# Routed FFN: fixed blocks for each expert's first 128 rows, the last two loads of w2 behind the last transpose

## The chip, the cores and the metric

One core of a Trainium2 chip. The metric is the device time of one execution in microseconds (us). The engines: PE (TensorE), DVE (VectorE), ACT (ScalarE), POOL (GpSimd) and SP (SyncE), which here only issues DMAs and waits.

## What is computed

The reference is a layer with a cross attention and a routed feed-forward part, for 1024 rows x of 128 values and 6404 rows of context. Cut to what matters:

```python
cq = jnp.einsum('bcd,bqd,d->bcq', c, q, w_cq) + b_cq          # c = layernorm(x), q = context
s = (c @ w_c + b_c)[:, :, None] + (q @ w_q + b_q)[:, None, :] + cq
a = jax.nn.softmax(s, axis=2)
c2q = jnp.einsum('bcq,bqd->bcd', a, q)
b_att = jax.nn.softmax(jnp.max(s, axis=2), axis=1)
q2c = jnp.einsum('bc,bcd->bd', b_att, c)[:, None, :]
x = x + jnp.concatenate([c, c2q, c * c2q, c * q2c], axis=-1) @ W_l.T + b_l
y = layernorm(x)
expert_id = argmax(y @ wr + br)                                # 8 experts, one for each row
out = x + (gelu(y @ w1[expert] + b1[expert]) @ w2[expert] + b2[expert])   # 128 -> 512 -> 128
```

## The kernel before, in words

**Attention.** The 1024 rows are 8 tiles of 128 (T = 8). Of each tile the 6404 scores are worked off in 7 pieces of 1024 columns (the last of 260). All products run in fp16 with a high and a low part, so that each operand is split in two. For a piece PE makes the scores (`scores`, L1059 to L1061), DVE takes them out of PSUM with their maximum (L800), ACT makes the exponential (L651) and its fp16 high part (`high`, L666), DVE or, for piece 3 of a tile, POOL makes the low part (`low`, L817; `low_piece`, L533), SP issues a DMA transpose of both parts (`transpose`, L393), and PE multiplies the transposed piece with the context (`weighted`, L1079 and L1081). Four buffers hold pieces under way; ACT's high part waits until the transpose of the piece four before it has landed.

**Weights.** w1 and w2 are loaded in 4 DMAs each of 512 KB (`load_w1`, `load_w2`). SP issues them between transposes: `W1_BEHIND` and `W2_BEHIND` name the tile and piece behind which. The loads of w2 stand behind pieces (2,5), (3,3), (4,1) and (4,5). POOL makes the high and low part of each of the 8 loads: `split(n)` has 4 casts (L570) and 4 subtractions (L574) of 128x256, placed behind its low piece of a tile by `splits`; the semaphore `w_low` counts the splits that are done.

**Behind the last transpose** SP writes an empty slot into every row of a DRAM buffer `xs` (14 blocks of 128 rows x 257 words, 5 DMAs, L431: "fills"); `slots_emptied` counts them.

**Routing** of the first 7 tiles (TA = 7). PE makes the router's scores, DVE the best expert of each row (`best`, L930 to L941), PE the rank of a row within its expert and the count of each expert, and DVE from them, in a chain in which every instruction waits for the one before (`link`), the slot of each row: L947 to L957, which ends with `pos_ready`. Each expert's rows fill whole blocks of 128, one expert behind the other, so 14 blocks (NB = 14) suffice whatever the counts, and which expert a block has is known only at run time. Then DVE normalises the last tile (`normalise`, L743 to L762). POOL waits for the fills and for `pos_ready` (L599, L600) and sends the 7 tiles' rows to their slots with 7 indirect DMAs (L602), counted by `rows_sent`. SP waits for that (L456) and reads the blocks back in 4 batches (`block_rows`, L449: the normalised halves first, the rest separately).

**The feed-forward part** has 22 blocks of 128 rows, in a fixed order. 8 of them are "dense": the last tile's 128 rows go through all 8 experts, with a mask, because they need no routing. They stand at places 0 to 4, 10, 16 and 21 (`DENSE_AT`); the 14 routed ("sent") blocks fill the other places (`SENT_AT`), the first of them at place 5. A dense block k takes its weights from the array `wp`. For a sent block SP reads the block's expert into a register and copies that expert's 512 KB from `wp` to a buffer (`fetch`, L444, SBUF to SBUF), the first two before the rows are read and the others among the reads. PE goes through the blocks: `up` (16 matmuls, L1276 to L1279), ACT's two Gelus (L710, L711), DVE's low part (L985), `down` (L1290 to L1296), DVE's sum (`finish_half` and `finish`). `up` is issued two blocks ahead. Before the first sent block's `up`, PE transposes the first batch of rows (`turn(0)`, L1245), ACT and DVE split it (L700, L977). PE waits for all splits (L1303) before the first dense block. POOL sends each sent block's result to `out` with an indirect DMA (L608) and at the end waits for all (L612); SP writes the last tile (L476) and waits for that (L477).

Of the kernel before, what the change touches and what calls it, by code (L numbers as in the profile page):

```python
# [24 lines left out]
F16 = mybir.dt.float16  # L25
I32 = mybir.dt.int32
# [7 lines left out]
def build(nc, x, ctxT, w3, b3, wlT, b_l, wr, br, w1, b1, w2, b2, out):  # L34
# [47 lines left out]
    with es:  # L82
# [6 lines left out]
        tri = sb("tri", [P, E, E])  # L89
# [52 lines left out]
        kedge = sb("kedge", [P, E, TA])  # L142
        slot_no = sb("slot_no", [P, NB, E])
        row_no = sb("row_no", [P, 1])
        token = sb("token", [P, T], I32)
        wc2 = gh[:, 0:2 * D].bitcast(F32)
        x_re = stageT[:, XRE:XRE + N].rearrange("p (t d) -> p t d", d=D)
# [3 lines left out]
        ints = stageT[:, XRE - NB * E:XRE].bitcast(I32)  # L151
# [17 lines left out]
        more = carve(E * TA).rearrange("p (a b) -> p a b", b=TA)  # L169
        below = carve(E * E).rearrange("p (a b) -> p a b", b=E)  # L170
        rank = carve(TA * E).rearrange("p (a b) -> p a b", b=E)
        cand = carve(T * E).rearrange("p (a b) -> p a b", b=E)
        mask = carve(E)
        chosen = carve(NB // 2, F16)
        past = carve(NB * E).rearrange("p (a b) -> p a b", b=E)
        oneh = carve(TA * E // 2, F16).rearrange("p (a b) -> p a b", b=E)
        nblk, sblk, eblk = carve(E), carve(E), carve(E)
        posf, rmx, bexpf = carve(TA), carve(T), carve(NB)
        pos, bexp = carve(TA, I32), carve(NB, I32)
# [11 lines left out]
        y7 = stageT[:, (NB + RING) * D:(NB + RING + E) * D].rearrange("p (e d) -> p e d", d=D)  # L191
# [70 lines left out]
        w_low = sem("w_low")  # L262
        b12_landed = sem("b12_landed")
# [9 lines left out]
        block_w_landed = [sem(f"block_w_landed{k}") for k in range(WSLOTS)]  # L273
# [87 lines left out]
        def block_w(b):  # L361

            k = b % WSLOTS
            return spare[k // (WSLOTS // 2)][:, k % (WSLOTS // 2) * 4 * F:(k % (WSLOTS // 2) + 1) * 4 * F]\
                .rearrange("p (a f) -> p a f", f=F)

        @block.sync
        def _(sp):
# [50 lines left out]
            W2_BEHIND = {(2, 5): 0, (3, 3): 1, (4, 1): 2, (4, 5): 3}  # L419
# [7 lines left out]

            sp.wait_ge(empty_ready, 2)
# [34 lines left out]
            fetch(4)  # L463
# [9 lines left out]
            for b in range(10, NB):  # L473
                fetch(b)
# [874 lines left out]
```

## Time and profile before

| | us |
|---|---|
| median of 3 runs | 234.27 |
| lowest and highest | 232.66 and 235.13 |
| the profiled execution's own time | 234.39 |
| its span, first to last instruction | 232.7 |
| busy in it: PE, DVE, ACT, POOL | 201.1, 180.6, 157.9, 128.6 |

The profile is of one execution. Times in its rows are us from the start of the span; an instruction's line is that of kernel.py. The span is shorter than the execution by what lies around it, 1.7 us. "Granted clock" is TensorE's: 1.00 stands for 2.4 GHz, 0.50 for 1.2 GHz. PE's busy time is of pipelined matmuls and says little by itself: what counts in each stretch is which wait ends last.

### The profile page before, as it was taken

Reading aid. Unit: us, or ns where it says so; the run is one execution under the profiler, and the core shown is the slowest. Engines: PE = TensorE matmul, PEld = TensorE weight load, DVE = VectorE, ACT = ScalarE, POOL = GpSimd, SP = SyncE. Lnnn points to the kernel's source line nnn. Section 1 sums busy time; section 2 is a strip of 40 time slices with the busy share of each in tenths; the row PEclk is TensorE's granted clock in tenths of the full one; section 3 lists DMA queues with packets and bytes.
Section 4 is the critical chain, followed back from the end, with each engine's and each line's share of the span. In section 5 each row is a group of like instructions: output and inputs, shape, how many; then the busy total and the mean of one; then the engine's idle time right before and its main releaser. Section 6 shows DMA issues by size and latency. Waiting matters only on the chain.

```text
span 232.7 us, 5011 instructions
## 1 busy us (share of the span) xinstructions
PE 201.1 (86%) x1837; PEld 150.3 (65%) x1837; DVE 180.6 (78%) x395; ACT 157.9 (68%) x249; POOL 128.6 (55%) x177
## 2 busy tenths in 40 slices
PE   0379969999999999989989899899993797999980
PEld 0133417776766767757666566789973686899970
DVE  2899797697998998998995997958756435776872
ACT  2752899399399699699595799689531445667650
POOL 3695718807915807978508947744400740066763
PEclk9999985899999999999999999999996569999998
DMA  6999979899999999999999999988994369999200
GB/s 215 389 251 263 226 223 237 192 234 174 220 215 216 278 230 269 241 198 233 216 213 256 184 220 258 201 196 185 239 263 121 120 219 290 346 370 378 98 11 12
DMA packets 142958, 51.78 MB, mean 223 GB/s; under 512 B 121172, under 2 KB 140773, under 8 KB 142934
## 3 DMA queue, kind: packets, MB, share of 16 engines
q1 hardware_dynamic: 142000, 50.08, 93.2%
q0 software_dynamic: 784, 1.38, 1.7%
q8 instruction: 14, 0.23, 0.4%
q14 instruction: 10, 0.08, 0.1%
q10 hardware_dynamic: 150, 0.00, 0.0%
HBM read 10.74 MB, written 3.75 MB: 62 GB/s over the span
## 4 chain that ended last, share of the span: by engine, by line
PE 49%; DVE 21%; DMA 11%; issue 8%; ACT 4%; POOL 3%; SPq 2%; DVEq 0%; POOLq 0%
DMA PT<-Phl 10%; PE psX L1079 5%; PE psS L1061 5%; PE psO L1079 5%; PE psS L1060 5%; PE psS L1059 5%; DVE S L800 5%; DVE Phl L817 3%; PE psS L1290 3%; PE psX L1081 3%; PE psO L1081 3%; ACT S L651 3%; SPq L393 2%; PE psS L1276 2%; PE psS L1296 2%
## 5 line engine op out<-in xcount | busy, mean ns | idle before, releaser
L651 ACT ACTIVATE S<-S,negb 128x1024 f32<-128x1024 f32 x48 | 55.1, 1147 | 18.4 <-DVE negb L808 18.4
L800 DVE TENSOR_SCALAR_CACHE_REDUCE S<-psS 128x1024 f32<-128x1024 f32 x48 | 58.2, 1217 | 11.4 <-PE psS L1061 11.2
L817 DVE TENSOR_TENSOR Phl<-S,Phl 128x1024 f16<-128x1024 f32 x38 | 51.5, 1355 | 5.0 <-ACT Phl L666 4.8
L533 POOL TENSOR_TENSOR Phl<-S,Phl 128x256 f16<-128x256 f32 x40 | 26.3, 689 | 51.7 <-ACT Phl L666 51.7
L666 ACT CAST Phl<-S 128x1024 f16<-128x1024 f32 x48 | 50.3, 1047 | 5.2 <-DMA PT<-Phl 3.7
L1059 PE MATMUL psS<-qT,gh 128*128 128x512 f16 x96 | 37.7, 393 | 5.4 <-DVE S L800 2.6
L1079 PE MATMUL psX<-qn,PT 128*128 128x256 f16 x204 | 36.4, 273 | 2.1 <-DMA PT<-Phl 2.1
L1079 PE MATMUL psO<-qn,PT 128*128 128x256 f16 x204 | 37.3, 276 | 0.9 <-DMA PT<-Phl 0.8
L1061 PE MATMUL psS<-qT,gl 128*128 128x512 f16 x96 | 37.9, 395 | 0.0
L1060 PE MATMUL psS<-qT,gh 128*128 128x512 f16 x96 | 37.9, 394 | 0.0
L1081 PE MATMUL psO<-qn,PT 128*128 128x128 f16 x204 | 35.7, 221 | 0.0
L1081 PE MATMUL psX<-qn,PT 128*128 128x128 f16 x204 | 35.0, 219 | 0.0
L608 POOL DMA_INDIRECT out_x<-stageT,S x14 | 17.7, 1265 | 22.1 <-DVE stageT L1011 17.1
L1079 PEld LDWEIGHTS psX<-qn,PT 128*128 128x128 f16 x204 | 20.0, 98 | 7.5 <-DMA PT<-Phl 3.5
L1079 PEld LDWEIGHTS psO<-qn,PT 128*128 128x128 f16 x204 | 20.3, 99 | 6.3 <-DMA PT<-Phl 1.9
L710 ACT ACTIVATE Phl<-psS 128x512 f16<-128x512 f32 x22 | 13.2, 598 | 15.4 <-PE psS L1279 9.0
L1081 PEld LDWEIGHTS psO<-qn,PT 128*128 128x128 f16 x204 | 20.2, 99 | 2.2 <-issue 0.3
L1081 PEld LDWEIGHTS psX<-qn,PT 128*128 128x128 f16 x204 | 20.0, 98 | 1.9
L1059 PEld LDWEIGHTS psS<-qT,gh 128*128 128x128 f16 x96 | 9.8, 102 | 14.6 <-DVE S L800 3.5
L1061 PEld LDWEIGHTS psS<-qT,gl 128*128 128x128 f16 x96 | 9.7, 101 | 12.1 <-issue 1.4
L985 DVE TENSOR_TENSOR Phl<-Phl 128x512 f16<-128x512 f32 x22 | 15.0, 682 | 2.4 <-issue 2.4
L574 POOL TENSOR_TENSOR wp<-wp 128x256 f16<-128x256 f32 x16 | 15.6, 1005 | 0.3
(239 smaller groups left out, 425.3 us busy)
## 6 DMA issues: line engine op xcount, KB each, us to landing
PT<-wp SPq DMA_DIRECT2D x8, 512.0 KB, 6.0
stageT<-in_ctxT SPq DMA_DIRECT2D x6, 512.0 KB, 7.0
qn<-wp SPq DMA_DIRECT2D x6, 512.0 KB, 7.3
wp<-in_w SPq DMA_DIRECT2D x4, 512.0 KB, 4.9
stageT<-in_w SPq DMA_DIRECT2D x4, 512.0 KB, 4.9
rows_by_expert<-stageT SPq DMA_DIRECT2D x4, 385.5 KB, 5.6
PT<-Phl SPq DMA_TRANSPOSE x48, 4.2
S<-rows_by_expert SPq DMA_DIRECT2D x2, 258.0 KB, 5.4
```

What stands on the lines that cost most here:

```text
L533: last = nc.gpsimd.tensor_tensor(lo[:, r], slot(t, e)[:, r], hi[:, r], ALU.subtract)
L574: last = nc.gpsimd.tensor_tensor(parts[:, 1, at + a:at + a + CHUNK], src[:, a:a + CHUNK], parts[:, 0, at + a:at + a + CHUNK], ALU.subtract)
L608: pool.indirect_dma_start(out=out, out_offset=bass.IndirectOffsetOnAxis(ap=rows[:, b, 2 * D:ROW].bitcast(I32), axis=0), in_=yf[:, b, :], i ...
L651: nc.scalar.activation(slot(t, e), slot(t, e), ACT.Exp, bias=negb[:, t:t + 1], accum_out=Lp[:, t * NG + e:t * NG + e + 1]).then_inc(exp_do ...
L666: nc.scalar.copy(hi, slot(t, e)).then_inc(high_done, 1)
L800: nc.vector.tensor_scalar(out=into, in0=bank(u, n)[:, 0:into.shape[1]], scalar1=1.0 / GS, scalar2=None, op0=ALU.mult, op1=ALU.max, accum_o ...
L817: nc.vector.tensor_tensor(lo, slot(t, e), hi, ALU.subtract).then_inc(low_done, 1)
L1059: nc.tensor.matmul(dst, g_h, hi, start=True, stop=False)
L1060: nc.tensor.matmul(dst, g_h, lo, start=False, stop=False)
L1061: last = nc.tensor.matmul(dst, g_l, hi, start=False, stop=True)
L1079: nc.tensor.matmul(acc[:, 0:2 * D].rearrange("p (a d) -> p a d", a=2), PT[:, 2 * e * TW + i, :], both[:, :, i, :], start=(j == 0), stop=Fa ...
L1081: last = nc.tensor.matmul(acc[:, 0:D], PT[:, 2 * e * TW + n + i, :], both[:, 0, i, :], start=False, stop=(j == QT - 1), skip_group_check=True)
```

## The change

Each expert's first 128 rows get a block of their own, at a fixed place: the first 8 sent blocks are those of experts 0 to 7, and take their weights and biases from where the dense blocks take them. The rows of an expert beyond 128 go to 6 further blocks (NX = 6), for which the expert is found and its weights are fetched as before; 14 sent blocks and 22 blocks remain. So 6 fetches are left of 14, each with a buffer of its own, and they come behind the first batches of rows. A row's slot is now its rank plus 128 times its expert, or, from rank 128 on, plus the expert's shift: the DVE chain from the counts to `pos_ready` is longer for this.

The loads 2 and 3 of w2 leave tile 4 and are issued behind the last transpose, ahead of the fills; load 2 goes to the place of `c_sb`, hence SP's wait for `q2c_in_psum`. Their high parts are made by ACT, in two casts of 128x1024 behind the transposed rows' copies (L687); their low parts by POOL, 4 subtractions each, the one ahead of the scatters of rows (and of the waits in front of them), the other behind them. POOL's other splits move: one in each of the tiles 1 to 6. PE waits for the four loads of w1 before the first dense block, and in `down` for the load of w2 that it uses. Of the dense blocks the one at place 16 moves to place 20, so that the last two blocks are dense and the sent ones end with place 19.

The core of the diff (renamed buffers, constants' patterns and the reuse of `y7` left out):

```diff
@@ -51,13 +51,12 @@
-    NB = TA + E - 1
+    NX = TA - 1
+    NB = E + NX
...
-    DENSE_AT = (0, 1, 2, 3, 4, 10, 16, 21)
+    DENSE_AT = (0, 1, 2, 3, 4, 10, 20, 21)
...
-    ROUTE_CONSTS = 19
-    WSLOTS = 12
-    FIRST = 2
+    ROUTE_CONSTS = 21
@@ -358,11 +360,14 @@
-def block_w(b):
-    k = b % WSLOTS
-    return spare[k // (WSLOTS // 2)][:, k % (WSLOTS // 2) * 4 * F:(k % (WSLOTS // 2) + 1) * 4 * F]\
-        .rearrange("p (a f) -> p a f", f=F)
+def w2_stage(k):
+    return c_flat if k == H - 2 else stageT[:, k * WC:(k + 1) * WC]
+def block_w(k):
+    half = (NX + 1) // 2
+    return spare[k // half][:, k % half * 4 * F:(k % half + 1) * 4 * F].rearrange("p (a f) -> p a f", f=F)
...
 def _(sp):
@@ -401,7 +406,7 @@
     def load_w2(k):
...
-        sp.dma_start(stageT[:, k * WC:(k + 1) * WC].rearrange("p (e k d) -> p e k d", k=FC, d=D),
+        sp.dma_start(w2_stage(k).rearrange("p (e k d) -> p e k d", k=FC, d=D),
@@ -416,7 +421,7 @@
-    W2_BEHIND = {(2, 5): 0, (3, 3): 1, (4, 1): 2, (4, 5): 3}
+    W2_BEHIND = {(2, 5): 0, (3, 3): 1}
@@ -425,23 +430,23 @@
+    sp.wait_ge(q2c_in_psum, 1)
+    load_w2(H - 2)
+    load_w2(H - 1)
...
-    expert_reg = [sp.alloc_register(f"expert{j}") for j in range(NB)]
-    sp.wait_ge(w_low, T)
+    expert_reg = [sp.alloc_register(f"expert{j}") for j in range(NX)]
...
-    sp.reg_load(expert_reg[0:FIRST], bexp[0:1, 0:FIRST])
-    ex = [sp.snap(r, min_val=0, max_val=E - 1) for r in expert_reg[0:FIRST]]
-    def fetch(b):
-        if b >= WSLOTS:
-            sp.wait_ge(y_in_psum, SENT_AT[b - WSLOTS] + 1)
-        sp.dma_start(block_w(b), wp[:, :, bass.ds(ex[b] * F, F)]).then_inc(block_w_landed[b % WSLOTS], 16)
+    sp.reg_load(expert_reg[0:NX], bexp[0:1, 0:NX])
+    ex = [sp.snap(r, min_val=0, max_val=E - 1) for r in expert_reg]
+    def fetch(k):
+        sp.dma_start(block_w(k), wp[:, :, bass.ds(ex[k] * F, F)]).then_inc(block_w_landed[k], 16)
     def block_rows(g, a, b, done):
@@ -449,31 +454,23 @@
-    for b in range(FIRST):
-        fetch(b)
-    sp.reg_load(expert_reg[FIRST:NB], bexp[0:1, FIRST:NB])
-    ex += [sp.snap(r, min_val=0, max_val=E - 1) for r in expert_reg[FIRST:NB]]
...
     block_rows(0, 0, D, rows_landed)
     block_rows(1, 0, D, rows_landed)
+    block_rows(0, D, ROW, rest_landed)
+    block_rows(1, D, ROW, rest_landed)
+    block_rows(2, 0, D, rows_landed)
+    sp.wait_ge(w_low, T)
+    fetch(0)
+    block_rows(2, D, ROW, rest_landed)
+    fetch(1)
+    block_rows(3, 0, D, rows_landed)
...
-    block_rows(0, D, ROW, rest_landed)
-    fetch(3)
-    block_rows(1, D, ROW, rest_landed)
-    fetch(4)
-    fetch(5)
-    block_rows(2, 0, D, rows_landed)
-    fetch(6)
-    block_rows(2, D, ROW, rest_landed)
-    fetch(7)
-    fetch(8)
-    block_rows(3, 0, D, rows_landed)
-    fetch(9)
     block_rows(3, D, ROW, rest_landed)
-    for b in range(10, NB):
-        fetch(b)
+    for k in range(3, NX):
+        fetch(k)
...
-    sp.dma_start(out[TA * P:N, :], y7[:, E - 1, :]).then_inc(out7_landed, 16)
+    sp.dma_start(out[TA * P:N, :], y7[:, (E - 1) % 2, :]).then_inc(out7_landed, 16)
@@ -559,6 +557,19 @@
+    def low_half(n, parts, src, at):
+        for a in range(0, WC, CHUNK):
+            last = nc.gpsimd.tensor_tensor(parts[:, 1, at + a:at + a + CHUNK], src[:, a:a + CHUNK],
+                                           parts[:, 0, at + a:at + a + CHUNK], ALU.subtract)
+        last.then_inc(w_low, 1)
+    def split_late(n):
+        at = (n - H) * WC
+        pool.wait_ge(w_high_late, n - T + 3)
+        low_half(n, w2p, w2_stage(n - H), at)
     def split(n):
@@ -582,7 +590,7 @@
     split(0)
-    splits = {2: (1,), 3: (2, 3), 4: (4,), 5: (5, 6), 6: (7,)}
+    splits = {2: (1,), 3: (2,), 4: (3,), 5: (4,), 6: (5,)}
@@ -595,12 +603,14 @@
+    split_late(T - 2)
     pool.wait_ge(tokens_ready, 1)
...
     for t in range(TA):
         pool.indirect_dma_start(out=xs, out_offset=bass.IndirectOffsetOnAxis(ap=pos[:, t:t + 1], axis=0),
...
+    split_late(T - 1)
@@ -685,6 +695,11 @@
+    for n in (T - 2, T - 1):
+        at = (n - H) * WC
+        act.wait_ge(w_landed[n], 16)
+        act.wait_ge(w_low, H)
+        nc.scalar.copy(w2p[:, 0, at:at + WC], w2_stage(n - H)).then_inc(w_high_late, 1)
     deviation(4, TA, T)
@@ -943,24 +958,30 @@
+    link(nc.vector.tensor_copy(extra[:, E:E + 1], ones[:, 0:1]))
...
-    link(nc.vector.tensor_tensor(more[:, :, :], count_psum.unsqueeze(2).broadcast_to([P, E, TA]),
+    link(nc.vector.tensor_tensor(more[:, :, :], count_psum.unsqueeze(2).broadcast_to([P, E, NX]),
...
-    link(nc.vector.tensor_reduce(out=nblk[:, :], in_=more[:, :, :], axis=AX.X, op=ALU.add))
+    link(nc.vector.tensor_reduce(out=extra[:, 0:E], in_=more[:, :, :], axis=AX.X, op=ALU.add))
...
-                                 nblk[:, :].unsqueeze(1).broadcast_to([P, E, E]), ALU.mult))
-    link(nc.vector.tensor_reduce(out=sblk[:, :], in_=below[:, :, :], axis=AX.X, op=ALU.add))
-    link(nc.vector.tensor_tensor(rank[:, :, :], rank_psum.rearrange("p (t e) -> p t e", e=E),
-                                 sblk[:, :].unsqueeze(1).broadcast_to([P, TA, E]), ALU.add))
+                                 extra[:, :].unsqueeze(1).broadcast_to([P, E, E + 1]), ALU.mult))
+    link(nc.vector.tensor_reduce(out=shift[:, :], in_=below[:, :, :], axis=AX.X, op=ALU.add))
+    ranks = rank_psum.rearrange("p (t e) -> p t e", e=E)
+    link(nc.vector.scalar_tensor_tensor(out=over[:, :, :], in0=ranks, scalar=float(P),
+                                        in1=shift[:, :].unsqueeze(1).broadcast_to([P, TA, E]),
+                                        op0=ALU.is_ge, op1=ALU.mult))
+    link(nc.vector.scalar_tensor_tensor(out=rank[:, :, :], in0=iob.broadcast_to([P, TA, E]), scalar=float(P),
+                                        in1=ranks, op0=ALU.mult, op1=ALU.add))
+    link(nc.vector.tensor_tensor(rank[:, :, :], rank[:, :, :], over[:, :, :], ALU.add))
...
     normalise(x1, x2n, TA, T, x2n_ready)
-    link(nc.vector.scalar_tensor_tensor(out=eblk[:, :], in0=nblk[:, :], scalar=float(P), in1=sblk[:, :],
+    link(nc.vector.scalar_tensor_tensor(out=eblk[:, :], in0=extra[:, 0:E], scalar=float(P), in1=shift[:, :],
...
-    link(nc.vector.tensor_tensor(past[:, :, :], eblk[:, :].unsqueeze(1).broadcast_to([P, NB, E]),
+    link(nc.vector.tensor_tensor(past[:, :, :], eblk[:, :].unsqueeze(1).broadcast_to([P, NX, E]),
@@ -1247,16 +1268,13 @@
     def weights(b):
-        if b in SENT_AT:
-            return block_w(SENT_AT.index(b))
-        k = DENSE_AT.index(b)
-        return wp[:, :, k * F:(k + 1) * F]
+        j = SENT_AT.index(b) if b in SENT_AT else DENSE_AT.index(b)
+        return wp[:, :, j * F:(j + 1) * F] if j < E else block_w(j - E)
     def bias_rows(b):
-        if b in SENT_AT:
-            return chosen[:, SENT_AT.index(b):SENT_AT.index(b) + 1].broadcast_to([P, P])
-        return pick[:, DENSE_AT.index(b), :]
+        j = SENT_AT.index(b) if b in SENT_AT else DENSE_AT.index(b)
+        return pick[:, j, :] if j < E else chosen[:, j - E:j - E + 1].broadcast_to([P, P])
     def up(b):
@@ -1264,8 +1282,9 @@
-            pe.wait_ge(block_w_landed[j % WSLOTS], 16 * (j // WSLOTS + 1))
-            pe.wait_ge(chosen_rows, 1)
+            if j >= E:
+                pe.wait_ge(block_w_landed[j - E], 16)
+                pe.wait_ge(chosen_rows, 1)
@@ -1286,6 +1305,8 @@
         pe.wait_ge(h_high, b + 1)
+        j = SENT_AT.index(b) if b in SENT_AT else DENSE_AT.index(b)
+        pe.wait_ge(w_low, H + j // 2 + 1 if j < E else T)
@@ -1300,7 +1321,7 @@
-    pe.wait_ge(w_low, T)
+    pe.wait_ge(w_low, H)
```

## Rows read from the trace of the kernel before

**Rows 1.** The page's first line.
```profile
span 232.7 us, 5011 instructions
```

**Rows 2.** PE's waits from 193 to 229 us, first row (in total, times, longest).
```profile
PE psS L1276 <- DVE S L977: 1.5, 2, 1.2
```

**Rows 3.** Four stretches, each from one tile's maximum to the next tile's.
```profile
core 0: us, PE busy (x) PEld busy (x) DVE busy (x) ACT busy (x) POOL busy (x), PEclk, DMA share, GB/s
79.50:96.11 16.61, 16.61 (x145) 11.76 (x143) 15.80 (x27) 14.17 (x21) 8.68 (x13) 1.00 1.14 244
96.11:113.38 17.27, 16.51 (x141) 11.27 (x138) 15.80 (x27) 14.17 (x21) 15.23 (x22) 1.00 1.11 231
113.38:132.03 18.65, 17.08 (x142) 11.42 (x141) 15.55 (x27) 14.17 (x21) 9.76 (x16) 1.00 1.23 209
132.03:148.63 16.60, 16.18 (x147) 11.97 (x148) 15.04 (x27) 14.17 (x21) 11.71 (x18) 1.00 1.19 234
```

**Rows 4.** The chain that ended last, inside tile 5 (start, us, what).
```profile
126.35 6.06 DMA PT<-Phl
```

**Rows 5.** ACT in order of time, the same place.
```profile
126.52 1.05 ACT L666 CAST Phl<-S 128x1024 f16<-128x1024 f32 x1 [2.68 <-DMA PT<-Phl]
```

**Rows 6.** SP in order of time: last load of w2, last tile's result.
```profile
118.84 0.57 SPq L404 DMA_DIRECT2D stageT<-in_w  x1
...
228.49 0.36 SPq L476 DMA_DIRECT2D out_x<-stageT  x1
```

**Rows 7.** Two stretches (columns as in rows 3): the load of x, the fills.
```profile
2.50:4.10 1.60, 0.00 (x0) 0.00 (x0) 0.00 (x0) 0.83 (x2) 0.54 (x1) 1.00 1.14 350
170.50:176.50 6.00, 5.47 (x50) 4.75 (x47) 2.50 (x12) 1.30 (x3) 0.20 (x1) 0.96 1.06 282
```

**Rows 8.** The fills' issues; us to landing of the last fill and last result.
```profile
L431 SPq DMA_DIRECT2D rows_by_expert<-stageT x5: 481/757/1392, 169.2 to 172.4; - x5
...
rows_by_expert<-stageT SPq DMA_DIRECT2D x1, 257.0 KB, 6.6
...
out_x<-stageT SPq DMA_DIRECT2D x1, 64.0 KB, 1.6
```

**Rows 9.** POOL in order of time: a split's subtractions, first scatter, last result.
```profile
146.30 3.72 POOL L574 TENSOR_TENSOR wp<-stageT,wp 128x256 f16<-128x256 f32 x4
...
180.29 1.21 POOL L602 DMA_INDIRECT rows_by_expert<-qT,S  x1 [9.11 <-DVE S L957]
...
228.33 0.98 POOL L608 DMA_INDIRECT out_x<-stageT,S  x1 [0.31 <-issue]
```

**Rows 10.** DVE in order of time: a small sum, and the chain's slots.
```profile
149.42 0.63 DVE L887 TENSOR_TENSOR Mrow<-mx,row_term 128x8 f32<-128x8 f32 x1
...
177.94 0.23 DVE L950 TENSOR_TENSOR S<-tri,S 128x64 f32<-128x64 f32 x1
...
179.20 0.17 DVE L957 CAST S<-S 128x7 int32<-128x7 f32 x1
```

**Rows 11.** PE in order of time: first dense block, first batch of rows, first sent block.
```profile
182.39 0.27 PE L1276 MATMUL psS<-S,wp 128*128 128x128 f16 x1 [0.84 <-DVE S L966]
...
193.72 0.55 PE L1245 MATMUL psX<-idf,S 128*128 128x128 f32 x3
195.43 0.23 PE L1276 MATMUL psS<-S,PT 128*128 128x128 f16 x1 [1.16 <-DVE S L977]
```

**Rows 12.** Stretches (columns as in rows 3): idle, what followed, dense blocks, idle.
```profile
30.20:32.30 2.10, 0.00 (x0) 0.00 (x0) 2.10 (x4) 2.08 (x3) 0.00 (x0) 1.00 0.35 130
33.00:42.50 9.50, 9.50 (x37) 6.19 (x36) 7.27 (x10) 7.85 (x13) 6.56 (x9) 0.50 1.07 234
...
176.00:189.50 13.50, 8.26 (x74) 7.34 (x74) 6.95 (x34) 4.39 (x9) 7.36 (x7) 0.50 0.47 157
...
193.80:195.40 1.60, 0.47 (x3) 0.23 (x3) 1.57 (x4) 1.10 (x3) 0.00 (x0) 1.00 1.04 346
```

More of the change, by code:

```diff
@@ L141, in build @@
         iota_e = sb("iota_e", [P, E])
-        kedge = sb("kedge", [P, E, TA])
-        slot_no = sb("slot_no", [P, NB, E])
+        kedge = sb("kedge", [P, E, NX])
+        slot_no = sb("slot_no", [P, NX, E])
         row_no = sb("row_no", [P, 1])
@@ L166, in build @@
         rows = carve(NB * ROW).rearrange("p (b w) -> p b w", w=ROW)
-        more = carve(E * TA).rearrange("p (a b) -> p a b", b=TA)
-        below = carve(E * E).rearrange("p (a b) -> p a b", b=E)
+        more = carve(E * NX).rearrange("p (a b) -> p a b", b=NX)
+        below = carve(E * (E + 1)).rearrange("p (a b) -> p a b", b=E + 1)
         rank = carve(TA * E).rearrange("p (a b) -> p a b", b=E)
+        over = carve(TA * E).rearrange("p (a b) -> p a b", b=E)
         cand = carve(T * E).rearrange("p (a b) -> p a b", b=E)
         mask = carve(E)
-        chosen = carve(NB // 2, F16)
-        past = carve(NB * E).rearrange("p (a b) -> p a b", b=E)
+        chosen = carve(NX // 2, F16)
+        past = carve(NX * E).rearrange("p (a b) -> p a b", b=E)
         oneh = carve(TA * E // 2, F16).rearrange("p (a b) -> p a b", b=E)
-        nblk, sblk, eblk = carve(E), carve(E), carve(E)
-        posf, rmx, bexpf = carve(TA), carve(T), carve(NB)
-        pos, bexp = carve(TA, I32), carve(NB, I32)
+        extra, shift, eblk = carve(E + 1), carve(E), carve(E)
+        posf, rmx, bexpf = carve(TA), carve(T), carve(NX)
+        pos, bexp = carve(TA, I32), carve(NX, I32)
         parts_ring = Phl[:, :, :, :].rearrange("p r a w -> p (r a w)")
@@ L272, in build @@
         rest_landed = [sem(f"rest_landed{g}") for g in range(len(BATCHES))]
-        block_w_landed = [sem(f"block_w_landed{k}") for k in range(WSLOTS)]
+        block_w_landed = [sem(f"block_w_landed{k}") for k in range(NX)]
         chosen_rows = sem("chosen_rows")
@@ L514, in _ @@
             numbers(iota_e[:, :], E, [[1, E]])
-            numbers(kedge[:, :, :].rearrange("p e k -> p (e k)"), E * TA, [[0, E], [P, TA]])
-            numbers(slot_no[:, :, :].rearrange("p b e -> p (b e)"), NB * E, [[P, NB], [0, E]])
-            then(nc.gpsimd.memset(tri[:, :, :], float(P)))
-            then(nc.gpsimd.affine_select(out=tri[:, :, :], in_=tri[:, :, :], compare_op=ALU.is_gt, fill=0.0, base=0,
+            numbers(kedge[:, :, :].rearrange("p e k -> p (e k)"), E * NX, [[0, E], [P, NX]], base=P)
+            numbers(slot_no[:, :, :].rearrange("p b e -> p (b e)"), NX * E, [[P, NX], [-P, E]], base=(E - 1) * P)
+            then(nc.gpsimd.memset(tri[:, :, 0:E], float(P)))
+            then(nc.gpsimd.affine_select(out=tri[:, :, 0:E], in_=tri[:, :, 0:E], compare_op=ALU.is_gt, fill=0.0, base=0,
                                          pattern=[[1, E], [-1, E]], channel_multiplier=0))
+            numbers(tri[:, :, E], E, [[-P, E]], base=(E - 1) * P)
             then(nc.gpsimd.memset(ones16[:, :], 1.0))
@@ L572, in split @@
                 pool.wait_ge(w_high, n + 1)
-                for a in range(0, WC, CHUNK):
-                    last = nc.gpsimd.tensor_tensor(parts[:, 1, at + a:at + a + CHUNK], src[:, a:a + CHUNK],
-                                                   parts[:, 0, at + a:at + a + CHUNK], ALU.subtract)
-                last.then_inc(w_low, 1)
+                low_half(n, parts, src, at)
             low_piece(1, 3)
@@ L1013, in finish @@
                 k = DENSE_AT.index(b)
-                nc.vector.scalar_tensor_tensor(out=y7[:, k, :], in0=half, scalar=mask[:, k:k + 1], in1=t,
+                nc.vector.scalar_tensor_tensor(out=y7[:, k % 2, :], in0=half, scalar=mask[:, k:k + 1], in1=t,
                                                op0=ALU.mult, op1=ALU.add).then_inc(y_ready, 1)
```

10 lines of the change are left out of this document (6 added, 4 removed).

## The prediction

> **What bounds the kernel now.** I read the end first. From the first sent block at 195.43 [rows 11] PE goes from block to block until it drains; its waits there [rows 2] are 1.5 us for DVE's split of the row batches, and the view's one other row is 1.0 us for DVE's low part. No row names a transfer: PE never waited for a fetch. So the 8 fetches that fall away give nothing by themselves on PE, and what counts is when that first sent block starts.
>
> It starts when the rows have come. With the last dense block done PE transposes the first batch at 193.72 and then idles 1.16 us for ACT and DVE [rows 11]. The batch is read when the 7 scatters have landed, and these begin at 180.29, 0.9 us after the slots are ready at 179.37 [rows 9, 10]. The fills are close by: the last, issued at 172.4, lands 6.6 us later, at 179.0 [rows 8]. So before the change DVE's chain sets the scatters, by 0.4 us.
>
> Then the loop: from one tile's maximum to the next takes 16.61 and 16.60 us in two stretches and 18.65 in the one that holds the last load of w2 [rows 3, 6]. The chain of waits lies there in a transpose's landing of 6.06 us [rows 4], for which ACT waited 2.68 us [rows 5]: the load stands in the transposes' queue.
>
> **The change part by part.** The sum is made against the profiled execution, 234.39 us (span 232.7 [rows 1] and 1.7 around it); the median is 234.27.
>
> *Loads out of the loop.* Loads 2 and 3 of w2 leave tile 4. The slow stretch should fall to the others' time: 18.65 - 16.60 = 2.05 us. From below: nothing, if the lateness has another cause. From above: 2.7, if the 17.27 of the stretch ahead, which holds load 2, also falls to 16.60 (0.67 more) [rows 3]. I take 2.05, since ACT's 2.68 us wait is a direct witness for the one stretch and I have none for the other. POOL loses one split in the loop, some 6 us, and was not waited for.
>
> *The loads in their new place.* Each of the two issues costs SP 0.57 us [rows 6], which is not the point: the queue is. They stand ahead of the five fills, and the engines are full while the fills run (share 1.06, 282 GB/s [rows 7]). The loads are 1.05 MB. At the rate of the load of x, which also has rows of 512 bytes, 350 GB/s [rows 7], they take 3.0 us; at the fills' own 282, 3.7 us. I take 3.2, near the like transfer. The last fill then lands at 182.2 (182.0 to 182.7) instead of 179.0. From below: nothing, if reads of DRAM and the writes of fills run beside each other.
>
> *The slot chain.* One copy and two operations of 56 elements are added, each as long as its like, some 0.25 us from start to start [rows 10]: 0.75 us. Slots are ready at 180.1. This also delays the last tile's normalisation and so the dense blocks (from 182.39 [rows 11] to 183.1). Both are hidden if the fills come last: POOL waits for both, and the later decides.
>
> *Scatters.* The first begins 0.9 us after the last of its waits, so at 182.2 + 0.9 = 183.1, against 180.29: 2.8 us late. The 7 scatters, the read, the transpose and the split follow at their old pace, so the first sent block is at 198.2. If only the chain counted, it would be 0.75 us.
>
> *ACT's casts.* Two of 1.05 us [rows 5], behind the copies of the transposed rows. The engines are free for the loads from some 170.5 on [rows 7], and at 1.5 to 1.9 us each, with a margin of two for the landing, they are there at 174 and 176; ACT is free again at 177, and its next work, the root for the last tile, comes after the slots at 179.37 [rows 10]. Hidden; were they later, each us past 179.4 would move the dense blocks, which the wait for the rows covers.
>
> *POOL's subtractions.* 3.7 us for four [rows 9]. The first set runs from some 175 to 178.7 and is done before the slots; behind it wait the scatters, not before 182.2. Hidden by the fills; without the fills' delay it would be hidden by 1.4 us. The second set runs behind the scatters, some 192.5 to 196.2. The weights of experts 0 to 5 are complete by then, and PE needs no others up to place 11; place 12, seven blocks behind the first sent one, comes well after 205. SP's fetches wait for it, behind five reads; the first is needed at place 14. Hidden.
>
> A rule bears on the first set. DVE's sum over 8 columns took 0.63 us at 149.42 while POOL's subtractions ran to 150.0, against 0.23 us for 64 columns with POOL idle [rows 9, 10]. The Trainium skill says why (SBUF — State Buffer, section "Who interferes with whom"): a DVE instruction with two inputs in SBUF contends with a GpSimd instruction that reads SBUF, and the second to issue waits for the first. The trace agrees. By it the three or four such operations of DVE's chain before 178.7 would each lose some 0.4 us, an estimate from these rows, and the slots would come at about 181.4; the first scatter would follow at 182.3, still ahead of the fills' 183.1. It makes nothing worse in my sum, and takes most of the gain from the rival in which the fills are not late.
>
> *The end.* Before, the last result of a sent block is issued by POOL at 228.33, for 0.98 us [rows 9]; at the landing time of the last tile's result, 1.6 us [rows 8], it is there at 230.9. The last tile's own, issued at 228.49 [rows 6], is there at 230.1. With both last blocks dense the sent results end a block, some 1.4 us, earlier, and the last tile's is the last: 0.8 us gained at most, nothing if the rest of the end is fixed. I take 0.7.
>
> Sum: 234.39 - 2.05 + 2.8 - 0.7 = 234.44. With the median 0.12 below the profiled execution, about 234.4 us: three terms that nearly cancel. By their ends the forecast's own range is 232.9 (loop 2.7, scatters 2.6, end 0.8 and a little) to 236.9 (loop nothing, late 3.2, end 0.7).
>
> **The rivals.**
>
> *The clock falls in the wait for the rows: slower.* The dense blocks end at 194 to 195, the first batch is transposed at some 196.5, the first sent block starts at 198.2. So PE has about 3 to 4 us with 0.5 us of work in them; before, it had 1.6 us with 0.47 us of work and stayed at 2.4 GHz [rows 12]. After 2.1 us without any work (30.2 to 32.3) it was at 1.2 GHz from 33 to 42.5, and it was low again from 176 to 189.5, with the dense blocks running on it [rows 12]. Against it: the case before stayed high, and the late dense blocks shorten the idle time. Price: at half the clock a block takes twice its time, so half of the time spent low is lost. In the rows the low level lasted for 7 to 10 us of work; 3.4 to 7.2 us low cost 1.7 to 3.6. The time is 236.1 to 238.0; I name 237.2. It decides from some 4.4 us at the low level on: half of that, 2.2 us, lifts the sum over 236.6.
>
> *The fills are not late.* Reads and writes run beside each other, or the loads are through before the fills fill the engines. Then DVE's chain sets the scatters, 0.75 us late: 234.39 - 2.05 + 0.75 - 0.7 = 232.4, and 231.7 with the whole 2.7 us of the loop. For it: the chain is the later one before. Against: the engines are full from 170.5 to 176.5 with fills alone [rows 7], and the margin is 0.4 us.
>
> *The loop gives nothing.* The stretch of 18.65 us comes from the two earlier loads of w2, which stay, and the loads' going only moves the lateness. Then 234.4 + 2.05 = 236.5. Against it: the stretch after it, without loads, takes 16.60 at once.
>
> *The change doesn't do what it says*: if a fixed block's weights came late, PE would wait in a product for the second set of subtractions. By the times above it is 9 us early; I give this no share.
>
> **How the numbers follow.** Forecast 0.40; clock 0.27; fills not late 0.20; loop gives nothing 0.13. A measurement of this kernel tells about 1%, 2.3 us, from no change, so faster is below 231.9 and slower above 236.6. Forecast: 0.05 faster, 0.31 same, 0.04 slower. Clock: 0.01, 0.03, 0.23. Fills: 0.10, 0.10, 0. Loop: 0.01, 0.03, 0.09. Sums: 0.17 faster, 0.47 same, 0.36 slower. The range leaves out less than a tenth at each end: the fills' rival down to 231.6, the clock's up to 238.3.
>
> **What would show it.** Right: the stretch that was 18.65 us is about 16.6; the last fill lands some 3 us later against the slots; POOL's first scatter begins behind the fills' landing and not behind L957's successor; PE's gap in front of the first sent block is longer by 1.5 us or more. The clock's rival: a granted clock of 0.50 after that gap. Wrong: the first scatter 0.9 us after the slots, or the stretch still over 18 us.

## The result, and the profile after

The change takes 249.38 us (median of 4 runs) against 234.63 us beside it: ratio 1.064 (1.056 to 1.072), 14.8 us slower. The forecast of 234.4 us, its range and every rival missed it. (Here and below the ratios leave disturbed runs out, so that one can differ from that of the medians.) The profiled execution took 248.52 us, its span is 246.8.

Page of the kernel after: the granted clock in 40 slices; the chain's shares by engine; two of the costliest groups; the loop's transposes (how many, median us from issue to landing).

```profile
PEclk9999999998999999997999999999998559999997
...
PE 40%; DMA 25%; DVE 17%; SPq 8%; issue 5%; POOL 2%; ACT 2%; DVEq 0%; ACTq 0%; POOLq 0%
...
L676 ACT CAST Phl<-S 128x1024 f16<-128x1024 f32 x48 | 50.2, 1045 | 18.3 <-DMA PT<-Phl 17.1
...
L1100 PE MATMUL psX<-qn,PT 128*128 128x256 f16 x204 | 39.0, 285 | 10.1 <-DMA PT<-Phl 10.1
...
PT<-Phl SPq DMA_TRANSPOSE x48, 4.9
```

The same line of the page before:

```profile
PT<-Phl SPq DMA_TRANSPOSE x48, 4.2
```

The loss is a wait for transposes. ACT's high parts waited 17.1 us for their landing and PE's products in the row shown 10.1 us; before, 3.7 and 2.1. DMA has 25% of the chain (11% before), SP's queue 8% (2%). The clock is not the cause: its mean is 0.952, against 0.944 before.

Timeline of the kernel after, rows of SP, POOL, DVE and PE from the last tile on (start, duration, engine, line, operation; in brackets the idle time ahead and what ended it):

```profile
179.27 1.77 SPq L398 DMA_TRANSPOSE PT<-Ptail  x1
181.09 0.57 SPq L409 DMA_DIRECT2D c_sb<-in_w  x1
181.72 0.57 SPq L409 DMA_DIRECT2D stageT<-in_w  x1
...
191.92 0.17 DVE L978 CAST S<-S 128x7 int32<-128x7 f32 x1
...
196.20 1.21 POOL L611 DMA_INDIRECT rows_by_expert<-qT,S  x1 [6.96 <-DMA rows_by_expert<-stageT]
...
209.24 0.55 PE L1266 MATMUL psX<-idf,S 128*128 128x128 f32 x3 [0.79 <-DMA S<-rows_by_expert]
210.95 0.23 PE L1295 MATMUL psS<-S,wp 128*128 128x128 f16 x1 [1.17 <-DVE S L998]
```

SP is through with the transposes at 181.04 us, before the change at 169.17: 11.9 us, all lost by the end of the loop. Behind it things go in the order that the forecast had. The scatters begin 4.1 us behind the slots, released by the fills ([rows 9, 10]: 0.9 behind, released by DVE); from the slots, 192.09, to the first sent block it is 18.86 us against 16.06, so 2.8 us more. From the first sent block to the end it is 35.85 us against 37.27.

What is odd stands at the start. Windows of both kernels over 16 to 20 us, where SP issues nothing but the transposes of the context and nothing has been changed, then two of the loop's tiles and the first sent blocks after (us; busy time and count for each engine; granted clock, DMA share, GB/s):

```profile
16.00:20.00 4.00, 3.66 (x18) 1.50 (x17) 4.00 (x7) 0.21 (x1) 4.00 (x6) 1.00 1.22 272
```

```profile
16.00:20.00 4.00, 4.00 (x15) 1.57 (x14) 3.22 (x8) 0.20 (x1) 3.86 (x7) 1.00 1.13 219
81.73:101.95 20.22, 17.33 (x143) 11.40 (x141) 15.37 (x27) 14.15 (x21) 8.88 (x14) 1.00 1.10 202
101.95:123.35 21.40, 18.04 (x141) 12.41 (x142) 15.16 (x27) 14.14 (x21) 7.48 (x12) 0.92 1.13 204
...
209.00:213.00 4.00, 2.60 (x32) 2.31 (x33) 1.25 (x3) 2.42 (x5) 0.00 (x0) 1.00 1.13 318
```

The transfer engines are busy throughout in both (share 1.22 and 1.13) and move 219 GB/s instead of 272. A queue order cannot do that ahead of the loop, so I looked for what the diff changes there. It is one number in the kernel's first allocation, `tri = sb("tri", [P, E, E])`, now `[P, E, E + 1]`: 288 bytes per partition instead of 256. (The cut of the diff ahead of the prediction does not show this line.) Allocations follow each other, so wp, qT, qn, S, Phl, PT and stageT, which all began at multiples of 256 bytes, now begin 32 bytes behind one. Theory A: that alone slows the transposes. Theory B: the moved loads, casts and splits upset the loop. Theory C: some of both.

### The profile page after: what moved, and what is told of

Same layout as the page of the kernel before. It is cut to its first block, busy times and chain, and to the rows that moved or that the text cites. A ratio compares the mean times of both kernels' runs of the same rounds, so it can differ in the third digit from the quotient of the medians.

```text
span 246.8 us, 4988 instructions
## 1 busy us (share of the span) xinstructions
PE 201.7 (82%) x1837; PEld 149.2 (60%) x1837; DVE 179.9 (73%) x398; ACT 159.7 (65%) x251; POOL 122.1 (49%) x171
## 2 busy tenths in 40 slices
DMA packets 138734, 47.58 MB, mean 193 GB/s; under 512 B 121044, under 2 KB 136549, under 8 KB 138710
## 4 chain that ended last, share of the span: by engine, by line
PE 40%; DMA 25%; DVE 17%; SPq 8%; issue 5%; POOL 2%; ACT 2%; DVEq 0%; ACTq 0%; POOLq 0%
DMA PT<-Phl 18%; SPq L398 5%; PE psX L1100 5%; DVE S L815 5%; PE psS L1080 5%; PE psS L1081 4%; PE psS L1082 4%; DMA rows_by_expert<-stageT 4%; DVE Phl L832 3%; PE psS L1311 3%; PE psO L1100 3%; PE psX L1102 3%; POOL rows_by_expert L611 2%; ACT Phl L676 2%; PE psS L1317 2%
## 5 line engine op out<-in xcount | busy, mean ns | idle before, releaser
L676 ACT CAST Phl<-S 128x1024 f16<-128x1024 f32 x48 | 50.2, 1045 | 18.3 <-DMA PT<-Phl 17.1
L832 DVE TENSOR_TENSOR Phl<-S,Phl 128x1024 f16<-128x1024 f32 x38 | 49.2, 1295 | 14.4 <-ACT Phl L676 14.4
L1100 PE MATMUL psX<-qn,PT 128*128 128x256 f16 x204 | 39.0, 285 | 10.1 <-DMA PT<-Phl 10.1
L1100 PE MATMUL psO<-qn,PT 128*128 128x256 f16 x204 | 36.8, 273 | 6.0 <-DMA PT<-Phl 6.0
L1102 PE MATMUL psX<-qn,PT 128*128 128x128 f16 x204 | 37.4, 227 | 0.0
L1082 PE MATMUL psS<-qT,gl 128*128 128x512 f16 x96 | 37.3, 389 | 0.0
L1100 PEld LDWEIGHTS psX<-qn,PT 128*128 128x128 f16 x204 | 20.8, 102 | 17.3 <-DMA PT<-Phl 13.0
L1100 PEld LDWEIGHTS psO<-qn,PT 128*128 128x128 f16 x204 | 19.9, 98 | 12.7 <-DMA PT<-Phl 9.1
L618 POOL DMA_INDIRECT out_x<-stageT,S x14 | 16.8, 1200 | 18.1 <-DVE stageT L1032 14.3
L1102 PEld LDWEIGHTS psX<-qn,PT 128*128 128x128 f16 x204 | 20.8, 102 | 1.7
L1102 PEld LDWEIGHTS psO<-qn,PT 128*128 128x128 f16 x204 | 20.0, 98 | 1.6
L1006 DVE TENSOR_TENSOR Phl<-Phl 128x512 f16<-128x512 f32 x22 | 15.9, 722 | 2.5 <-ACT Phl L726 2.5
L1295 PE MATMUL psS<-S,wp 128*128 128x128 f16 x64 | 15.1, 236 | 2.3 <-DVE S L998 1.5
```

The source lines that it names most:

```text
L618: pool.indirect_dma_start(out=out, out_offset=bass.IndirectOffsetOnAxis(ap=rows[:, b, 2 * D:ROW].bitcast(I32), axis=0), in_=yf[:, b, :], i ...
L676: nc.scalar.copy(hi, slot(t, e)).then_inc(high_done, 1)
L832: nc.vector.tensor_tensor(lo, slot(t, e), hi, ALU.subtract).then_inc(low_done, 1)
L1006: nc.vector.tensor_tensor(hp[:, i, 1, :], hf[:, i, :], hp[:, i, 0, :], ALU.subtract).then_inc(h_low, 1)
L1082: last = nc.tensor.matmul(dst, g_l, hi, start=False, stop=True)
L1100: nc.tensor.matmul(acc[:, 0:2 * D].rearrange("p (a d) -> p a d", a=2), PT[:, 2 * e * TW + i, :], both[:, :, i, :], start=(j == 0), stop=Fa ...
```

## The experiments

**Addresses, nothing else.** The pads are unused tensors of 4-byte numbers; the order of work stays. The kernel before, shifted as the change shifts it:

```diff
 tri = sb("tri", [P, E, E])
+sb("pad", [P, 8])
```

> Theory A (addresses): the change made the first tensor of the on-chip memory 32 bytes per partition longer, so every large tensor behind it starts 32 bytes off a multiple of 64, and the DMA transposes that read Phl and qT and write PT and qn are slower for that alone. Then the kernel before, with nothing changed but 32 bytes put behind tri, loses what the change lost up to the last transpose: its last transposes issue near 181 us instead of 169.2, and the time is 234.6 + 11.9 = 246.5 us (243 to 249), ratio 1.05. Theory B (order of work: the moved loads, casts and splits upset the loop): nothing of the order changes here, so 234.6 us, ratio 1.00. Theory C (the loop got slower from both): about half, 240 us.

Measured: 251.07 us, ratio 1.069 (1.061 to 1.077). The whole loss, in a kernel with none of the change. It is 2 us above the range expected, which was made from the loss up to the change's last transpose; here SP is through with the transposes at 184.1 us, not at 181.0.

The changed kernel with everything put back:

```diff
 tri = sb("tri", [P, E, E + 1])
+sb("pad", [P, 56])
```

> The changed kernel with 224 bytes put behind tri, so that every large tensor starts a multiple of 256 bytes from where it started before, as in the kernel before. Theory A: the transposes are at their old pace, the last ones issue at 169.2 - 2 = 167 us, and what is left is the working of the prediction: 234.4 us, ratio 1.00 (0.99 to 1.015). Theory B: the order of work is what slowed the transposes, so 248.5 us and ratio 1.06 stay. Theory C: 241 to 243 us.

Measured: 235.17 us, ratio 1.003 (0.999 to 1.006). With the addresses put back the change is no longer slower. Theories B and C fall.

As in the first, with 16 numbers for 8:

> The kernel before with 64 bytes put behind tri: the large tensors start at an odd multiple of 64. If theory A holds and a multiple of 64 is enough, 234.6 us, ratio 1.00; if it takes a multiple of 256, as all of them have in the kernel before, about as slow as with 32 bytes, 240 to 247 us. Theory B: 234.6 us.

Measured: 251.90 us, ratio 1.075 (1.063 to 1.086), above the 240 to 247 us expected: a multiple of 64 is not enough.

In the next kernel PT alone starts 32 bytes off; with the second pad, what lies behind it, stageT too, starts 64 bytes off.

```diff
+sb("pad", [P, 8])
 PT = sb("PT", [P, 2 * QT, P], F16)
+sb("pad2", [P, 8])
```

> The kernel before with 32 bytes ahead of PT and 32 behind it: only PT, which the 48 transposes of the loop write, starts 32 bytes off a multiple of 64; all that they read lies as before. Theory A, if the side that is written decides: 243 to 247 us. If the side that is read decides: 234.6 us. If both count: between, near 240 us. Theory B: 234.6 us.

Measured: 234.88 us, ratio 1.001 (0.998 to 1.005). Where the transposes write does not matter, 32 bytes off at least.

And what they read:

```diff
+sb("pad", [P, 8])
 Phl = sb("Phl", [P, PARTS, 2, GR], F16)
 Ptail = sb("Ptail", [P, 2, TAILP], F16)
+sb("pad2", [P, 8])
```

> The kernel before with 32 bytes ahead of Phl and 32 behind Ptail: what the loop's transposes read starts 32 bytes off a multiple of 64; PT, c_sb and all behind them start at a multiple of 64, and wp, qT, qn and S lie as before. Theory, after the run in which PT alone was shifted and nothing changed: the side that is read decides, and this kernel loses what the shift of everything lost, 16.7 us less the share of the first transposes of qT, so 248 to 251 us, ratio 1.06 to 1.07. Rival: it is another of the shifted tensors (S, wp or qT, which the engines or the loads use), then 234.4 us, ratio 1.00.

Measured: 251.79 us, ratio 1.070 (1.063 to 1.078). Where they read does. The windows of this kernel show it within one execution: qT lies well, and its transposes run at the old 272 GB/s; Phl lies badly, and the first of the tiles that are slow in the change takes 20.6 us.

```profile
16.00:20.00 4.00, 4.00 (x13) 1.52 (x12) 3.16 (x6) 0.20 (x1) 3.90 (x7) 1.00 1.24 272
81.73:102.37 20.64, 17.63 (x145) 11.44 (x143) 15.89 (x27) 14.15 (x21) 10.88 (x18) 1.00 1.13 203
```

All 17 traces agree, each tensor by its own address: from issue to landing the transposes of Phl take 4.1 to 4.3 us in the median where Phl starts at a multiple of 256 bytes and 4.9 to 5.1 where it does not, those of qT 4.1 to 4.2 and 4.7 to 5.1. That the engines work more slowly on a shifted tensor is no rival: ACT's cast, which writes Phl, takes 1045 to 1047 ns in all of them.

The changed kernel with a pad of 24 behind `tri`:

> The changed kernel with 96 bytes put behind tri: every large tensor starts at an odd multiple of 128. If a row slice of 128 elements, 256 bytes, is slow whenever it crosses a multiple of 256, this is as slow as the change itself: 249 us, ratio 1.06. If a multiple of 128 is enough: 235.2 us, as with 256.

Measured: 252.32 us, ratio 1.067 (1.058 to 1.075): 128 bytes off costs what 32 cost. Of the offsets tried only a multiple of 256 is fast.

**Which addresses in the changed kernel.** `after_Phl_only` puts back Phl and Ptail; `after_front_off` has the first pad alone and so puts back all behind them too.

```diff
+sb("pad", [P, 56])
 Phl = sb("Phl", [P, PARTS, 2, GR], F16)
 Ptail = sb("Ptail", [P, 2, TAILP], F16)
+sb("pad2", [P, 8])
```

> The changed kernel, with every tensor as far off as the change put it (32 bytes off a multiple of 64), but for Phl and Ptail, which get 224 bytes ahead of them and so start at a multiple of 256 again. If the address that the loop's transposes read from is the whole of the loss: 235.2 us, ratio 1.00, as with all addresses put back. If another tensor has a share: between 237 and 248 us. The 7 transposes of qT still cross: at most some 2 us.

Measured: one time of 235.87 us and three from 240.8 to 242.6, so I ran it again.

> The kernel of after_Phl_only once more, since its four times lay apart (235.87, and three from 240.8 to 242.6). In its profiled execution the last transpose was issued at 170.7 us (before 169.2, after the change 181.0), so the loop's loss was gone but for some 3 us; the fills landed 4.5 us behind the slots (3.2 with all addresses put back), and the granted clock fell to 0.50 in the wait for the rows, as in the rival of the prediction. Theory A: Phl is all of the loss, and the three times come from the clock alone: mostly 235 to 236 us. Theory B: the other addresses (qT's, read by the first 7 transposes; stageT's, read by the fills) cost 2 to 3 us more, and that brings the wait that drops the clock: 238 to 242 us again.

Measured: 238.23 us in the median of 13, from 234.9 to 242.9; ratio 1.012 (1.008 to 1.015), and 1.018 between the medians of all runs.

> The changed kernel with 224 bytes ahead of Phl alone: wp, qT, qn and S are 32 bytes off as the change left them, and Phl, PT and all behind them, stageT too, start at a multiple of 256. What differs from after_Phl_only is that the fills read from an aligned tensor and PT and c_sb lie as before. If the fills' address is what made after_Phl_only slow: 235.2 to 237 us. If qT's is (the first 7 transposes, some 1 to 2 us): as after_Phl_only, 238 to 242 us.

Measured: 237.54 us, ratio 1.011 (1.006 to 1.015), not told apart from Phl alone. By the ratios Phl's address is 5.2 of the 6.1 points between 1.064 and 1.003 (4.5 by the medians of all runs). PT and the fills' source had no price in `before_PT32` (1.001), where the scatters do not wait for the fills; in the changed kernel, where they do, the fills' share is not settled.

Where the last point lies is open. In `after_front_off` the 7 transposes of qT are slow again at the start, yet the first maximum comes no later for it (27.1 us, 27.6 in `after_aligned`). What its trace shows besides is the clock: PE waits 1.34 us for the rows, the clock falls to 1.2 GHz, and from the first sent block to the end it is 37.67 us against 35.74 in `after_aligned`. Its start and the 6 us from the first sent block, then these 6 us in `after_aligned`:

```profile
16.00:20.00 4.00, 4.00 (x16) 1.67 (x15) 3.36 (x6) 0.20 (x1) 3.46 (x6) 1.00 1.13 223
198.63:204.63 6.00, 6.00 (x67) 5.64 (x68) 1.71 (x5) 2.99 (x6) 0.00 (x0) 0.72 1.11 352
```

```profile
196.36:202.36 6.00, 5.71 (x84) 5.39 (x85) 3.34 (x9) 3.81 (x8) 0.00 (x0) 1.00 1.11 358
```

Nor is the spread of `after_Phl_only` settled. In both its profiled executions, with spans of 240.8 and 241.1 us, the clock was at 1.2 GHz for some 7 us in and behind PE's wait for the rows, 1.89 and 3.00 us, as in the forecast's first rival. The other runs left no trace; their mean granted clock is 0.965 and 0.969 in the two shortest, 0.938 to 0.951 in the five longest and mixed between.

**What is left of the forecast, at the old addresses.** The change now being 1.003, its parts can be taken one by one. `after_in_loop` puts the two loads back where they were:

```diff
-W2_BEHIND = {(2, 5): 0, (3, 3): 1}
+W2_BEHIND = {(2, 5): 0, (3, 3): 1, (4, 1): 2, (4, 5): 3}
...
-sp.wait_ge(q2c_in_psum, 1)
-load_w2(H - 2)
-load_w2(H - 1)
```

> The changed kernel with the old addresses, and with the last two loads of w2 back at their old places in tile 4 (into stageT, as before; DVE waits for the first late split ahead of its first dense result); casts, subtractions and fixed blocks stay as changed. By the prediction's steps the two halves of the move are given back: the loop is 2.4 us longer, and the fills land ahead of the slots again, so that the first scatter starts 0.9 us behind the slots and not 3.0, 2.1 us less: 235.2 + 2.4 - 2.1 = 235.5 us. If the loads were no reason for the late fills: 237.6 us. If leaving the loop gave nothing: 233.1 us.

Measured: 233.15 us, ratio 0.990 (0.986 to 0.993), the case in which leaving the loop gave nothing. The times show it: by the ratios the kernel is some 3 us faster with the loads back in the loop, 2.1 us of it at the scatters. (The traces alone would not: 118.53 us from the first maximum to the last, 118.57 in `after_aligned`, are of one execution each.) The scatters are what differs in the traces. First `after_aligned`, then `after_in_loop`, the last line of the slots and the first scatter:

```profile
177.98 0.17 DVE L979 CAST S<-S 128x7 int32<-128x7 f32 x1
...
181.20 1.21 POOL L612 DMA_INDIRECT rows_by_expert<-qT,S  x1 [6.52 <-DMA rows_by_expert<-stageT]
```

```profile
177.74 0.17 DVE L976 CAST S<-S 128x7 int32<-128x7 f32 x1
...
178.83 1.21 POOL L609 DMA_INDIRECT rows_by_expert<-qT,S  x1 [4.39 <-DVE S L976]
```

With the loads behind the last transpose the fills release the scatters, 3.05 us behind the slots' end; without them DVE does, 0.92 us behind.

`after_fixed_only` is `after_in_loop` with the splits of the last two loads of w2 back on GpSimd in the loop, so that the fixed blocks, with the lines that they add to the slot chain, and the order of the last blocks are all that remains.

```diff
-splits = {2: (1,), 3: (2,), 4: (3,), 5: (4,), 6: (5,)}
+splits = {2: (1,), 3: (2, 3), 4: (4,), 5: (5, 6), 6: (7,)}
```

> The kernel of after_in_loop with the last two quarters of w2 split by GpSimd in the loop, both halves, where the kernel before has them: what is left of the change is the fixed blocks, the order of the last blocks and the lines of the slots, at the old addresses. Theory A: the loop of after_in_loop was short (118.5 us from the first maximum to the last, against 122.2) since GpSimd's two splits had left it; put back they cost 3 us, so 236 us, ratio 1.00. Theory B: neither the loads nor the splits count in the loop, and its length differs from one profiled execution to the next; then 233.2 us, ratio 0.99, as without them.

> The kernel of after_fixed_only (233.02 us, ratio 0.987) once more, beside after_in_loop on the same chip. If GpSimd's two splits in the loop cost what the profiled executions said (its loop 120.3 us against 118.5, and 0.7 us of it given back in the slots): 1 us more than after_in_loop. If they cost nothing: the same.

> The kernel of after_in_loop (233.15 us, ratio 0.990) once more, beside after_fixed_only: the same 233 us, ratio 0.99, if the late splits gain nothing; 1 us less than after_fixed_only if they do.

Measured: 233.02 us, ratio 0.987 (0.982 to 0.991), and again 232.56, 0.993 (0.989 to 0.996), beside 232.97, 0.989 (0.984 to 0.995), for `after_in_loop_again`. The splits cost nothing that can be told. The lengths of the loop on which theory A of that expectation stood were chance: the two profiled executions of the very same `after_in_loop` have 118.5 and 122.1 us.

`after_one_behind` is `after_aligned` with the second late load behind the fills, and ScalarE's cast of it behind the last tile's copies (L708 to L710 in `after_aligned`).

```diff
 load_w2(H - 2)
-load_w2(H - 1)
 sp.wait_ge(empty_ready, 2)
 for k in range(FILLS):
...
+load_w2(H - 1)
```

> The changed kernel with the old addresses; of the two late loads of w2 the second goes behind the fills, and ScalarE casts it behind the last tile's copies. By the prediction's step on the fills half the bytes ahead of them are gone, so the last fill lands 1.6 us earlier against the last transpose, the first scatter starts 1.4 to 1.6 us earlier, and the time is 235.2 - 1.5 = 233.7 us. If the late fills had another cause: 235.2 us. If the second load comes too late for the blocks that use it: over 235.2 us, with a wait of PE or ScalarE for it in the profile.

Measured: 236.04 us, ratio 0.996 (0.990 to 1.001). The ratio is not told apart from the changed kernel's 1.003, and the reason expected is not there: the first scatter starts 3.5 us behind the slots (178.29 to 181.75), no earlier. The clock fell here too: PE waited 1.58 us for the rows, the granted clock was 0.72 over the next 6 us, and from the first sent block to the end it is 37.53 us. So this time is not the fills' alone.

`after_one_after` has a wait in front of that load:

```diff
+sp.wait_ge(slots_emptied, 16 * FILLS)
 load_w2(H - 1)
```

> The kernel of after_one_behind, in which SP waits for the fills to land before it issues the second late load. If that load, though behind the fills in the queue, took its share of the transfer engines from them, the fills now land some 1.9 us earlier against the last transpose (13 us behind its issue, not 15), the first scatter starts 1.9 us earlier, and the time is about 234.3 us, ratio 0.99. If the one load ahead of the fills makes all of the 3.7 us: as after_one_behind, 236.0 us, ratio 0.996 to 1.00. In both ScalarE waits for the late load, near 183 us, and the dense blocks start later.

Measured: 233.00 us, ratio 0.991 (0.987 to 0.996). Its timeline:

```profile
177.32 0.17 DVE L984 CAST S<-S 128x7 int32<-128x7 f32 x1
...
178.95 0.37 SPq L410 DMA_DIRECT2D stageT<-in_w  x1
...
179.80 1.21 POOL L613 DMA_INDIRECT rows_by_expert<-qT,S  x1 [5.16 <-DMA rows_by_expert<-stageT]
```

SP's issue at 178.95 marks the fills' landing: 14.1 us behind the last transpose's issue at 164.87. In `after_one_behind` the last fill, issued at 171.2 with 9.6 us to landing, is there at 180.8, 15.0 behind 165.81. So the load behind the fills took some 0.9 us from them, half of what I expected, and the one ahead 3.0 (14.1 against 11.1 before and in `after_in_loop`). These are of one execution each, and with both loads ahead it is 14.8, so the 0.9 is weakly shown.

## Why the prediction was wrong

*What failed.* No step of it has a term for addresses. The part "Loads out of the loop" took the other stretches' 16.60 us as what the loop would run at, that is, it took the transposes to keep their price; and "The slot chain" counted the operations that are added but not the wider `tri`, whose 32 bytes move every tensor behind it. The runs put 14 us on that: 1.064 against 1.003 with the addresses alone put back.

How it comes to so much can be worked out. A tile's transposes read 6 times 2048 slices of 128 elements, 256 bytes, and 768 of the tail: 3.34 MB. At 272 GB/s these are 12.3 us, at 219 GB/s 15.3 (estimates from the two windows). A tile took 16.6 us [rows 3], so by these estimates the first left 4.3 us for loads and waits, the second 1.3. That is why the loss does not simply stand in the transposes' own time: the last two tiles after took 16.6 us each, with nothing else in the queue, and the two shown took 20.2 and 21.4, with a load of w2 issued in or just ahead of them (88.72 and 101.22). The kernels with bad addresses and all four loads in the loop bear it out: their SP is through with the transposes at 184.1 to 184.4 us (`before_shift32`, `before_shift64`, `before_Phl32`), those with two loads left in it at 181.0 and 182.6 (`after`, `after_shift128`). There the loads' leaving was worth some 1.5 to 3 us, by one execution each.

The Trainium skill (DMA: Bandwidth & Descriptors, section "How a descriptor splits into AXI transactions") has the rule I should have weighed: a transaction must start from an address that is a multiple of 256 bytes. By it a slice of 256 bytes that starts elsewhere takes two transactions for one (worked out from its rule). The traces agree in kind: the slices that start at a multiple of 256 are fast, those at the three offsets tried slow. They do not agree with its count of beats, by which slices 32, 64 and 128 bytes off would cost 9, 10 and 12 beats for 8 (worked out from its rule): in the window of 16 to 20 us the three have 214 to 224, 216 and 221 GB/s, the same.

*The other steps*, read at the old addresses (`after_aligned`, 235.17 us; forecast 234.4):

- "Loads out of the loop", 2.05 us: wrong, nothing that shows. The rival in which the loop gives nothing had this right. ACT's wait of 2.68 us behind one load was real, but a stretch of one execution is no measure of it: the loop differs by 3.5 us between executions of one kernel. The trace before had a sign against the term: the stretch of 16.61 us, one of those to which the slow one should fall, holds loads of w2 itself, issued at 82.55 and 93.93.

```profile
93.93 0.57 SPq L404 DMA_DIRECT2D stageT<-in_w  x1
```

- "The loads in their new place" and "Scatters", 2.8 us: right. The last fill lands 14.8 us behind the last transpose instead of 11.1, so 3.7 us later (forecast 3.2), and the scatters start 0.9 us behind it, 3.3 us later against the last transpose. From the slots to the first sent block it is 18.2 us (16.06 before). The rows are not alone on this path: see the clock, below.
- "The slot chain", 0.75 us, hidden: right in both. From the last maximum to the slots it is 31.98 us against 30.74; without GpSimd's subtractions beside it (`after_fixed_only`) 31.45. So 0.7 us are the added lines and 0.5 the contention, where the estimate had three or four times 0.4. It stands in two operations whose inputs are both in SBUF, 0.62 and 0.35 us beside the subtractions (172.12 to 174.67) against 0.22 each without; one that reads PSUM as well (0.22) and a reduction (0.21) in the same time lost nothing. The Trainium skill (SBUF — State Buffer, section "Who interferes with whom") has it so: a DVE instruction with two SBUF inputs contends with a GpSimd instruction that reads SBUF.
- "ACT's casts" and "POOL's subtractions", hidden: right, but for that contention. No wait of PE or DVE ends with one of them.
- "The end", 0.7 us: right in kind, 1.5 us. From the first sent block to the end it is 35.74 us against 37.27. The cap of 0.8 was wrong: the span ends 4.4 us behind POOL's last issue in both (228.33 to 232.7, 227.66 to 232.1), where the forecast had 2.6.
- "The clock falls in the wait for the rows": it did not in the change. After the gap the clock is at 2.4 GHz. But the rival was real: the clock fell there in 6 of the 17 traces. In the five of these with the changed order it is 37.3 to 38.5 us from the first sent block to the end, and 35.7 to 36.1 in the seven in which it stayed: 1.3 to 2.8 us (priced at 1.7 to 3.6).
- PE's gap, which was to be longer by 1.5 us or more: it was not. PE waits 0.79 us for the rows in the change and not at all in `after_aligned`, since the dense blocks end 16.4 us behind the slots in both, 14.2 before. In one of the dense blocks PE waits for DVE's low part, 2.13 us in the change and 2.40 in `after_aligned`; DVE had been idle for over 5 us just before, which the profile ascribes to nothing on this core. That wait had no term either, and its cause is open.

Two slips of the working changed nothing: the low end of the range, by its own terms 234.39 - 2.7 + 2.6 - 0.8, is 233.5 and not 232.9, and POOL loses two splits in the loop, not one.

Without the loop's 2.05 us the sum would have been 236.5, and with the end at 1.5 us 235.7; measured is 235.2. So it is partly luck that the kernel at the old addresses comes so near 234.4. The fixed blocks with the new order of the last blocks gain 1% by themselves (0.987 and 0.993), of which the traces show 1.2 to 1.5 us from the first sent block to the end (36.06 and 35.74 against 37.27); which of the two gives it was not tried. The move of the loads costs 1.3% (0.990 to 1.003), that of the splits nothing that shows. The best versions here are `after_fixed_only`, `after_in_loop` and `after_one_after`, at the old addresses: 232.6 to 233.2 us, 1% below the kernel before and not told apart.

## What to carry to other kernels

Look at what an edit does to the addresses of every tensor allocated behind it, above all of those that a DMA transpose reads: keep them at multiples of 256 bytes, and compare transfer rates in a stretch that the change did not touch. Before a stretch of one execution carries a term of the sum, see whether the other executions have it too; here they differed by more than the term.

## What the hardware showed that I had not expected

- A DMA transpose whose source starts 32, 64 or 128 bytes off a multiple of 256 runs a fifth slower, whatever the offset: 214 to 224 GB/s in seven executions instead of 261 to 273 in ten. The destination's offset costs nothing (32 bytes: 1.001). The page counts 121,044 packets under 512 bytes, and the transposes' slices of 256 bytes are 117,504 (48 times 2048, 8 times 768, and 13,056 for the context): nearly every small packet is such a slice.
- A transfer issued ahead of others in the same queue delays them: the last fill lands 3.0 us later for 512 KB issued ahead of the five. One issued behind them seems to take from them too, 0.9 us. Both are of one execution of each kernel.
- The granted clock fell to 1.2 GHz around PE's waits for the rows in `after_Phl_only`, 1.89 and 3.00 us, and stayed there for some 7 us.
